# Edge passes of a graph network: expanded rows accumulated in one PSUM bank and copied by ScalarE, with hidden and edge banks doubled

## What is computed

```python
for l in range(5):
    h = _leaky(x @ W1[l] + b1[l]) @ W2[l] + b2[l]
    e = _leaky(edge_attr @ We1[l] + be1[l]) @ We2[l] + be2[l]   # 32 -> 64 -> 64
    msg = h[src] * e * dot_scale[l]
    agg = jax.ops.segment_sum(msg, dst, num_segments=n)
    out = x + agg * res_w[l]
    x = (out - mean) * rsqrt(var + LN_EPS) * ln_g[l] + ln_b[l]
```

## Time and profile before

| | us |
|---|---|
| median of 3 runs | 22706.24 |
| lowest, highest | 22622.63, 22733.8 |
| the profiled execution, own time | 22674.76 |
| its span, first to last instruction | 22672.7 |

### The profile page before, as it was taken

How to read it: one execution, slowest core, us unless ns; L and a number is a source line. 1 busy time by engine, 2 the same in 40 slices (tenths; PEclk the granted TensorE clock), 3 DMA queues, 4 the chain that set the end, 5 groups by cost and what they waited for, 6 DMA issues and landing times. The chain is left out here.

```text
span 22672.7 us, 329567 instructions
## 1 busy us (share of the span) xinstructions
PE 12966.2 (57%) x95507; PEld 10907.3 (48%) x95507; DVE 11406.3 (50%) x19693; ACT 5335.2 (24%) x10114; POOL 10006.5 (44%) x10482
## 2 busy tenths in 40 slices
PE   0344444556455666666566666666666666666465
PEld 0222223555345555555455555555555555555454
DVE  7544544444991121212555655565566556555413
ACT  0000000111443333333222222222222222222233
POOL 0455554665014434343455454445444544455342
PEclk9656665555557777778888887878887878778777
DMA  2111111111344434343222222222222222222343
GB/s 75 35 39 39 39 39 40 51 52 49 148 176 116 117 108 115 108 115 103 71 70 69 63 70 67 70 62 70 70 66 68 70 69 64 69 70 70 82 116 90
DMA packets 1284160, 1745.76 MB, mean 77 GB/s; under 512 B 576614, under 2 KB 828390, under 8 KB 1283174
## 3 DMA queue, kind: packets, MB, share of 16 engines
q1 hardware_dynamic: 960833, 1351.53, 19.9%
q0 software_dynamic: 317440, 348.12, 7.9%
q10 hardware_dynamic: 5040, 35.13, 0.4%
HBM read 1425.04 MB, written 308.76 MB: 76 GB/s over the span
## 5 line engine op out<-in xcount | busy, mean ns | idle before, releaser
L1133 POOL DMA_INDIRECT rows_buf<-feature_table,idx_buf x4960 | 4909.1, 990 | 4909.7 <-DMA idx_buf<-src_idx 3013.8
L857 POOL DMA_INDIRECT rows_buf<-feature_parts,idx_buf x2176 | 2054.4, 944 | 2878.2 <-PE banks L912 1897.8
L899 PE MATMUL banks<-sums_space,tmp 128*128 128x192 bf16 x13720 | 2090.6, 277 | 1602.1 <-issue 1109.7
L869 ACT ACTIVATE sums_space<-banks 128x384 bf16<-128x384 f32 x3920 | 1638.1, 452 | 3290.6 <-PE banks L886 2316.3
L886 PE MATMUL banks<-table_parts,tmp 128*128 128x192 bf16 x13720 | 2088.1, 276 | 299.5 <-DMA tmp<-one_hots 280.9
L899 PEld LDWEIGHTS banks<-sums_space,tmp 128*128 128x128 fp8e4 x13720 | 1333.0, 109 | 1869.2 <-issue 1831.8
L1180 PE MATMUL banks<-attr_buf,params 128*128 128x256 f32 x5420 | 1776.9, 454 | 782.9 <-ACT hidden L1145 354.6
L707 POOL DMA_INDIRECT rows_buf<-attention_table,idx_buf x1664 | 1571.9, 945 | 1455.7 <-DVE parts L1447 906.0
L1268 DVE TENSOR_REDUCE early<-banks 128x256 f32<-128x768 f32 (+1 forms) x1470 | 1253.6, 853 | 1861.9 <-remote 1482.3
L1150 ACT ACTIVATE sums_space<-onehot 128x448 bf16<-128x448 f32 (+1 forms) x1355 | 814.2, 601 | 5156.9 <-DVE onehot L1288 1442.6
L1192 PEld LDWEIGHTS banks<-params,hidden 128*128 128x128 f32 x10840 | 1768.0, 231 | 106.3 <-issue 39.0
(11 more groups left out here) (380 smaller groups left out, 22377.4 us busy)
## 6 DMA issues: line engine op xcount, KB each, us to landing
tmp<-one_hots SPq DMA_DIRECT2D x1715, 448.0 KB
one_hots<-tmp SPq DMA_DIRECT2D x245, 448.0 KB
attr_buf<-attr SPq DMA_DIRECT2D x760, 128.0 KB
attr_buf<-cell_attr SPq DMA_DIRECT2D x735, 128.0 KB
rows_buf<-feature_table,idx_buf POOLq DMA_INDIRECT x4960
gathered_rows<-rows_buf SPq DMA_DIRECT2D x208, 272.0 KB
rows_buf<-gathered_rows SPq DMA_DIRECT2D x208, 272.0 KB
rows_buf<-feature_parts,idx_buf POOLq DMA_INDIRECT x2176
```

Of the source, the lines that this page charges most:

```text
L857: pool.indirect_dma_start(out=far_rows[:, u, t, :], out_offset=None, in_=table3, in_offset=bass.IndirectOffsetOnAxis(ap=idx_buf[:, u, t:t ...
L869: act.activation(cell_rows[:, q, 0:width], bank[q][:, 0:width], ACT.Copy).then_inc(s_cells_sb, 1)
L899: ins = pe.matmul(bank[4 + h][:, half * 3 * D:(half + 1) * 3 * D], hot_buf[:, k, j, (2 + half) * P:(3 + half) * P], cell_rows[:, q, j % 2 ...
L1133: pool.indirect_dma_start(out=edge_rows[:, u, t, :], out_offset=None, in_=table, in_offset=bass.IndirectOffsetOnAxis(ap=idx_buf[:, u, t:t ...
```

## The change

- `expand` no longer writes 192 columns for each cell into two pairs of banks. The three parts of both source blocks are accumulated in the same 64 columns of a cell, and the 7 cells of a chunk stand side by side in bank 0. Where a cell had 2 matmuls of 192 columns it has 6 of 64.
- DVE's `cell_sums` are gone. ACT copies bank 0 to `cell_row` in one instruction (`copy_rows`), between the high part of the work before and the hidden layer of the work behind.
- The hidden layer has banks 4 and 5, the edge features banks 2 and 3, the far sums bank 1 alone, the strip's sums bank 6. The ring of bank pairs and its semaphore `s_free` are replaced by `s_row` and `s_taken`.
- In PE's turn n stand expand(n+2), then hidden_layer(n+4), edge_features(n+2), add_up(n). hidden_layer(n+4) waits for the copy of n+2, and edge_features(n+2) for the multiply of n. SP's turn n waits for hidden layer n+4.
- In DVE's turn the multiply and the one-hot stand first; taking the sum of the work two before and adding it to the accumulator stand together behind them, ahead of the rest of the high part.

```diff
-                for pos in range(3):
+                for pos in range(4):
                     next_attributes(work(0, pos))
                 with sp.Fori(0, HS // 2) as i:
                     for pos in range(TURN):
-                        turn(work(i, pos), work(i, pos + 3), False)
+                        turn(work(i, pos), work(i, pos + 4), False)
...
-                    act.activation(hidden[:, w.side, :], bank[4], ACT.Identity, bias=b1).then_inc(s_act_hid, 1)
+                    act.activation(hidden[:, w.side, :], hidden_bank(w), ACT.Identity, bias=b1).then_inc(s_act_hid, 1)
...
-                def turn(w_next, w_ahead):
+                def copy_rows(w):
+                    act.wait_ge(s_fill, w.chunk + 1)
+                    if not w.begins:
+                        act.wait_ge(s_mult, w.n - (0 if w.follows_near else 1))
+                    act.activation(cell_row[:, 0:CELLS, :].rearrange("p t d -> p (t d)"), expanded[:, 0:CELLS * D], ACT.Copy).then_inc(s_row, 1)
+
+                def turn(w_next, w_later, w_ahead):
                     if w_next:
                         high_part(w_next)
+                    if w_later and w_later.near:
+                        copy_rows(w_later)
                     if w_ahead:
                         copy_hidden(w_ahead)
                     if w_next:
                         middle_part(w_next)
...
-                    if not w.begins:
-                        pe.wait_ge(s_act_hid, w.n)
+                    if not early:
+                        pe.wait_ge(s_act_hid, w.n - 1)
...
-                    if not w.begins:
-                        pe.wait_ge(s_mult, w.n)
+                    if not early:
+                        pe.wait_ge(s_mult, w.n - 1)
...
-                    for part, cells in enumerate((range(0, 4), range(4, CELLS))):
-                        pe.wait_ge(s_free, w.op + (part + 1))
-                        pe.sem_inc(s_turn, 1)
-                        to = pair_of_banks(w.ring + part)
-                        for j in cells:
-                            for side in range(2):
-                                ins = pe.matmul(to[:, j % 4 * 2 * P:j % 4 * 2 * P + 3 * D], hot_buf[:, w.k, j, side * P:(side + 1) * P],
-                                                table_parts[:, 2 * (w.k * CELLS + j) + side, :], start=(side == 0), stop=(side == 1))
-                        ins.then_inc(s_fill, 1)
+                    pe.wait_ge(s_row, w.chunk + 1)
+                    pe.sem_inc(s_turn, 1)
+                    for j in range(CELLS):
+                        for side in range(2):
+                            for n in range(3):
+                                ins = pe.matmul(expanded[:, j * D:(j + 1) * D], hot_buf[:, w.k, j, side * P:(side + 1) * P],
+                                                table_parts[:, 2 * (w.k * CELLS + j) + side, n * D:(n + 1) * D],
+                                                start=(side == 0 and n == 0), stop=(side == 1 and n == 2))
+                    ins.then_inc(s_fill, 1)
...
-                        pe.wait_ge(s_free, w.op + 1)
+                        pe.wait_ge(s_taken, w.g + 1)
...
-                def cell_sums(w, part):
...
-                        dve.wait_ge(s_free, w.op + 4)
+                        dve.wait_ge(s_row, w.chunk + 2)
...
                 def turn(w_past, w_next, w_later, w_ahead):
+                    if w_next:
+                        multiply(w_next)
+                    if w_later and not w_later.near:
+                        one_hot(w_later)
                     if w_past:
                         take_sums(w_past)
-                    if w_next:
-                        multiply(w_next)
-                    if w_later and w_later.near:
-                        cell_sums(w_later, 0)
-                    elif w_later:
-                        one_hot(w_later)
+                        add_sums_of(w_past)
                     if w_next:
                         rest_of_high(w_next)
                     if w_ahead:
                         leaky(w_ahead)
-                    if w_later and w_later.near:
-                        cell_sums(w_later, 1)
                     if w_next:
                         low_part(w_next)
-                    if w_past:
-                        add_sums_of(w_past)
```

More of the change, by code:

```diff
@@ L83, in param_columns @@
     }
-Work = namedtuple("Work", "near n begins side op ring own adds added follows_near s k g u round tiles slot attr loads filled")
+Work = namedtuple("Work", "near n begins side own adds follows_near s k g u round tiles slot attr loads chunk")
 class Steps:
@@ L351, in build @@
         s_fill = sem("s_fill")
-        s_free = sem("s_free")
+        s_row = sem("s_row")
+        s_taken = sem("s_taken")
         numbers = [s.num for s in semaphores]
@@ L1038, in work, with count @@
             turns = 0 if tail else i
-            def count(counts, by):
-                return turns * by + counts[m] if m in counts else None
-            common = dict(n=i * TURN + pos, begins=isinstance(i, int) and i * TURN + pos == 0, side=pos % 2, op=count(op_of, OPS_A_TURN),
-                          ring=op_of[m] % 2, own=count(own_of, ADDS_A_TURN), adds=count(adds_of, ADDS_A_TURN), added=added_of.get(m, 0),
-                          follows_near=is_near(m - 1))
+            def count(counts):
+                return turns * ADDS_A_TURN + counts[m] if m in counts else None
+            common = dict(n=i * TURN + pos, begins=isinstance(i, int) and i * TURN + pos == 0, side=pos % 2,
+                          own=count(own_of), adds=count(adds_of), follows_near=is_near(m - 1))
             if f is None:
@@ L1048, in work, with edge_bank, hidden_bank @@
                 return Work(near=True, s=i * 2 + h, k=k, g=None, u=None, round=None, tiles=CELLS, slot=c % 2, attr=c % 2,
-                            loads=i * CHUNKS + (c // 2 + 1), filled=count(filled_of, FILLED_A_TURN), **common)
+                            loads=i * CHUNKS + (c // 2 + 1), chunk=i * 2 * CHUNKS + c, **common)
             per = 2 * (CHUNKS - 1)
             return Work(near=False, s=None, k=None, g=i * per + f, u=f % U, round=i * (per // U) + (f // U + 1), tiles=G, slot=f % 2,
-                        attr=2 + f % 2, loads=i * (per // 2) + (f // 2 + 1), filled=None, **common)
-        def pair_of_banks(n):
-            return banks[:, n % 2 * 2:n % 2 * 2 + 2, :].rearrange("p b e -> p (b e)")
+                        attr=2 + f % 2, loads=i * (per // 2) + (f // 2 + 1), chunk=None, **common)
         def hybrid_pass(block):
+            expanded, far_bank, strip_bank = bank[0], bank[1], bank[6]
+            def edge_bank(w):
+                return bank[2 + w.side]
+            def hidden_bank(w):
+                return bank[4 + w.side]
             w1, b1 = COLS["l2"](params, "We1"), COLS["l2"](params, "be1")
@@ L1191, in edge_features @@
                             t, at = 4 * half + 2 * pair, (2 * pair + half) * P
-                            ins = pe.matmul(bank[5][:, t * D:(t + 2) * D], hidden[:, w.side, at:at + P], w2,
+                            ins = pe.matmul(edge_bank(w)[:, t * D:(t + 2) * D], hidden[:, w.side, at:at + P], w2,
                                             start=False, stop=(half == 1 and pair == 1))
```

101 lines of the change are left out of this document (38 added, 63 removed).

## The result

| | us |
|---|---|
| kernel before, on the same chip, median of 4 runs | 22664.44 (22613.59 to 22733.8) |
| changed kernel, median of 4 runs | 22958.24 (22925.92 to 23021.99) |
| ratio after / before | 1.0131, 95% interval 1.0091 to 1.0171 |
| changed kernel, profiled execution and its span | 22941.21, 22939.2 |

The change makes the kernel 1.3% slower: 294 us by the medians, 267 us by the two profiled spans. The forecast was 372 us more.

What follows compares the result with a forecast made beforehand. Gather bursts on POOL were taken to hold back PE, counted in instructions: a group goes from 15.9 to 16.5 us, +0.6 x 620 = 372 us on 22675, plus 31 for the median: 23080 us, range 21800 to 23900.

Steps and rivals of the forecast that it cites:

- Step 1: PE's expansion: 42 matmuls of 64 columns for 14 of 192, 203 instructions a group, 0.1 us a chunk, hidden.
- Step 2: DVE's two reduces go, 2.0 us a group, 1254 us busy; the wait before them moves to ACT.
- Steps 3 and 6: ACT's copy, 0.577 us a chunk, costed at nothing (424 us if uncovered); SP's indices a turn later, nothing by itself.
- Step 4: Double banks, hidden layer one turn further ahead: one PE-DVE trip for two turns, worth 0 to 1020 us.
- Step 5: DVE's order: block-number load and two additions between multiply and rest of high part; 0 to 465 us, taken 0.
- 115 instructions a burst: PE during POOL's gather bursts: each lets through 115 instructions whatever their width, leaving 88 a group for the gap.
- the short side: Low estimate of an edge group's period: burst 10.0, hold 1.5, 88 instructions at 24 a us 3.7; 15.2 us.
- the pass at 7.3 ms: Long estimate, from a pass with 215 PE instructions and 17.1 us a group: 16.6 us, with 16.5 taken.
- The queue of 64: Skill page's TensorE queue of 64 instructions; some 64 of 128 in a 20 us burst would be queued, others retired.
- The reduces were the path: Rival, edge passes: bursts hold by time or columns, so the gap loses DVE's 2.0 us; -1240 us, 21470; 17%.
- Two turns of room: Rival, edge passes: PE always has input in the gap, 15.2 us a group; -434 us, 22270; 14%.
- ACT's queue turns into the wait: Rival: expansion stays in a burst, middle part waits behind copy_rows; +3.2 us a group, +1980 us, 24690; 6%.

Runs made afterwards that it cites:

- the change without the split: Changed kernel with 14 overlapping expansion matmuls of 192 columns a chunk in place of 42 of 64 (wrong values): 22571.57 us, ratio 0.9763 to the kernel before.
- the split: Kernel before with each 192-column expansion matmul issued as three of 64 columns into the same places: 24042.26 us against 23128.12, ratio 1.040.
- without bursts: One gather in place of eight per far group of the edge passes (wrong values): kernel before 19123.9 us, changed kernel 18271.45 us, ratios 0.8448 and 0.8071.
- with two: Kernel before, POOL waiting for its gathers to land after the fourth and eighth of each far group of the edge passes: 22659.54 us, ratio 0.980.
- with one pause: POOL waiting for its gathers after the fourth of each far group: kernel before 21177.55 us, ratio 0.9357; changed kernel 21352.41 us, ratio 0.9429.

## Why the prediction held, and where it was off

- **The mechanism and the sign** were right. A group became longer although DVE's work shrank, by 0.36 us (16.27 against 15.9) where 0.6 was taken. The five passes as a whole became 267 us longer (0.43 us a group), forecast 372.
- **Step 1, the expansion.** 203 instructions a group, as worked out. In a quiet stretch 42 matmuls take 1.39 us at 14023.42, where 14 of 192 took 1.32: 0.07 us more, taken as 0.1. (By the rule of "TensorE: Matmul & The Clock Gate", section "Back-to-back issue gap", in the Trainium skill, they would take 3.4 us, the prediction's estimate; the trace does not agree, and the 1600 us did not come.)
- **Step 2, the reduces.** Their wait came back on ACT, as said: 556.5 us of "remote" at L1150, and behind it 567.2 us at DVE's leaky.
- **Steps 3 and 6.** ACT's copy takes 0.538 us, taken as 0.577, and the time of the passes doesn't show it as work. Nothing in the trace points to SP's new turn.
- **Step 4, double banks and one trip for two turns,** and steps 2 and 3 with it, were mis-sized: no gain was taken for them apart. Together they gain 557 us, 0.90 us a group, by the change without the split. How much of it is the banks' and how much the reduces' was not taken apart.
- **Step 5, DVE's new order,** taken as 0: 0.3% by the middle values, not told from nothing. Only the place of the additions was tried, not that of the multiply and the one-hot.
- **The sum's terms.** "115 instructions a burst" held as a mean of single bursts before (112), but a double burst carries 157 for two groups, so the gaps of before carried 43 instructions a group and not 22. After, bursts carry more (129 single, 184 double, 92 a group), so of 203 instructions 105 pass in bursts and 98 in gaps, where the sum had 88. The gaps' growth is 55 instructions and not 66. The pace was the open term: the short side took 24 a us, the pass at 7.3 ms showed 12.6. Measured are 16, hence 6.1 us of gap where the forecast left 6.5. So the forecast lay near the result by a pace between its two sides, chosen and not derived, and the two wrong counts in it partly cancel. The 1.5 us of hold in the short side came from no row.
- **The sum from the experiments** has two measured terms, each in a kernel that had it alone: -0.90 for all but the split, +1.47 for the split, +0.57 us a group or 353 us. Together they came to 0.43 to 0.47 (267 and 294 us). The difference of 0.1 us is within the intervals of the two ratios.
- **The queue of 64.** The prediction saw agreement with the page's 64 in a count that stops at 128 in a burst of 20 us. That count is no ceiling: double bursts of the kernel before carry 106 to 221, those of the changed kernel 143 to 239. No run here shows where the instructions wait.
- **The rivals.** "The reduces were the path" is wrong here; without bursts, where DVE is 91% busy before, the change gains 4.5%. "Two turns of room" and the reduces together are a true gain of 0.90 us a group that the split outweighs; which of the two it is was not taken apart. "ACT's queue turns into the wait" happens in some bursts, as at 14004 to 14017, but its price of 3.2 us a group did not come.

What stays open: what in the chip holds PE back. The runs show that it comes with rows of gathers, that it is counted in instructions to a good part, and that it ends some 2 us after the last gather of a row. Whether it is the report of a finished matmul or the next instruction's start that is held can't be told from these traces, nor whether it comes from POOL's part of a gather or from the transfers that the gather starts, since one gather in place of eight removes both.

## What to carry to other kernels

Where an engine waits for a matmul that has long ended in the records, look at what POOL does just then; if it gathers in an unbroken row, try to let it wait once in a group for its own rows (13.2 us a group instead of 15.9), and not so often that POOL becomes the bound (15.3 with two). Beside such bursts price PE's work in instructions and not in columns: a split that adds no column and 0.07 us of PE cost 3.5 to 4.0% here. Here a saving on an engine that waited for a held signal moved the wait to the engine that reads that signal next.

## What the runs showed of the hardware that I had not expected

- Within a burst PE does not stop dead: its matmuls begin one or two at a time, 0.71 us apart (14009.15, 14009.86, 14010.58, 14011.28), where 42 of them take 1.39 us outside.
- One pause of 2.26 us in a group's row of gathers gains 1468 us over 620 groups, 2.4 us each, itself paid. In all passes that have such rows together it gains 13% of the kernel.
- After a hold PE can run at the lower of its two clock levels (1.2 of 2.4 GHz). The 42 matmuls of an expansion take 2.44 us at 14118.22, in a gap with a granted clock of 0.58, and 1.39 us at 14023.42. Ahead of the fall to the lower level at 14115.75 PE had begun only three matmuls since 14112.1, at 14113.47, 14114.17 and 14115.58, with POOL in the last gathers of the burst. Inside an edge pass the granted clock is 0.76 in the changed kernel, 0.83 with one pause, 0.97 without bursts. The row:

```profile
14118.22 2.44 PE L1202 MATMUL banks<-table_parts,tmp 128*128 128x64 bf16 x42
```
